# Attention on one NeuronCore: one batch of value matmuls for each chunk of queries, the column groups of TensorE holding the two halves of the keys

## The chip, the core and the metric

The kernel runs on one core of one Trainium2 chip. A core has a matrix engine (TensorE, PE in the profile; its weight loads are listed as PEld), VectorE (DVE), ScalarE (ACT), GpSimd (POOL) and SyncE (SP), which run beside each other and wait for one another by semaphores. Matrix products land in PSUM, which has eight banks of 512 fp32 columns; everything else on the chip lies in SBUF. The metric is the device time in microseconds of one execution; shown is the median of three.

## The reference

Two transformer layers over 4096 tokens of width 256. What the change touches is the attention of the first one, with 16 heads of width 16. The names `k` and `q` are exchanged in the scores, so the softmax of a row runs over what the code calls queries:

```python
q = _split_heads(x @ Wq.T + bq)
k = _split_heads(x @ Wk.T + bk)
v = _split_heads(x @ Wv.T + bv)
scores = jnp.einsum('hbnd,hbmd->hbnm', k, q) * SCALE
attn = jax.nn.softmax(scores, axis=-1)
out = jnp.einsum('hbnm,hbmd->hbnd', attn, v)
```

For each head this is a 4096 by 4096 matrix of scores, its row maxima, its exponentials, and their product with the values and with ones (numerator and denominator). The rest of the layer, and a second layer with linear attention and a mixture of 64 small experts, follow.

## The kernel before

`attention_phase` takes the heads in 8 pairs and the 4096 key columns in 8 blocks of 512 (`TB`), which makes 64 steps. In a step the 4096 query rows go by in 32 chunks of 128 (`MC`), numbered c. The two heads of a pair are e = 0 and e = 1. They live in different halves of the partitions of `QST` and `KST` (rows 0 to 63 and 64 to 127).

For each chunk TensorE does three things. `unit_a` (L624) makes scores with keys on the partitions, 128 by 512, for both heads, and does so ahead of time for a later block; DVE takes their maxima (L719), and the maxima of a whole block travel through POOL (`shift_parts`) and a DMA into two extra rows of `KST`. `unit_s` (L636) makes scores with queries on the partitions, the maxima subtracted by those extra rows; ACT takes their exponential (L696) into one of 8 slots of `PR`. There are only three PSUM banks for it (`SB`), so the matmul number v waits for the exponential number v-3 (`s_before`); from v = 3 to v = 4 the bank repeats at once, so number 4 of a step waits for exponential 3. `values` (L646) multiplies `PR` by the values and by ones (32 columns of weights, `VH`), which accumulates over the chunks in the one bank `PV`.

The order on TensorE is written out in `step`. In each q it issues S for head 0, two matmuls of A (head 1, head 0), and S for head 1. After every second q (odd ones) comes a batch of values for two older chunks: four matmuls of 512 columns that fill the four column groups of 32: head by chunk parity. These matmuls are in plain fp32, and the trace records each as two loads and two matmuls; A and S are of the type fp32r, and recorded once. At the end of a step `PV` holds even and odd chunks in different partitions. ACT copies it to `OS` (L707), POOL moves half of it to other partitions by DMA (L763), adds (L766) and stores it (L773).

The next step's first value matmul waits until `PV` has been copied (`pv_read`). `exp` waits with `p_free` until the slot of `PR` is free again, once for two chunks.

Of the kernel before, what the change touches and what calls it, by code (L numbers as in the profile page):

```python
# [13 lines left out]
F32 = mybir.dt.float32  # L14
# [6 lines left out]
P = 128  # L21
# [3 lines left out]
TB = 512  # L25
# [471 lines left out]
SCALE = 1.0 / D ** 0.5  # L497
LEAD = 8
EXPS = 2 * MC
PVS = MC // 2  # L500
S_BANKS = 3
K_SLOTS = 4
P_SLOTS = 8
# [14 lines left out]
def attention_phase(nc, d, K, V_all):  # L518
# [5 lines left out]
    with ExitStack() as ctx:  # L524
# [7 lines left out]
        PM = sb("PM", [P, 2, 2, TT, NB], F32)  # L532
        neg = sb("neg", [P, 2, 2 * TT], F32)
        NM = sb("NM", [P, 2, PARTS, 2 * TT], F32R)
        OS = sb("OS", [P, 2, TB], F32)
        OG = sb("OG", [P, TB], F32)
        O2 = sb("O2", [P, TB], F32)
        A = ps("A", [P, 4, TB])
        SB = ps("SB", [P, S_BANKS, TB])
        PV = ps("PV", [P, TB])  # L540
# [5 lines left out]
        p_free, os_free, pv_read = sem("p_free"), sem("os_free"), sem("pv_read")  # L546
        neg_ready, neg_high, neg_low = sem("neg_ready"), sem("neg_high"), sem("neg_low")
        shift_loaded = [sem(f"shift_loaded{i}") for i in range(2)]
        groups_moved, o_stored = sem("groups_moved", from_zero=True), sem("o_stored", from_zero=True)
        LOAD = 16 * 2 * len(K_PARTS)  # L550
        SHIFT = 16 * 2 * PARTS
        P_AHEAD = P_SLOTS // 4

        def in_steps(eng, body):

# [9 lines left out]
        with nc.Block() as block:  # L565
# [52 lines left out]
            @block.tensor  # L618
            def _(pe):
                def unit_a(u, e, nb, slot):  # L620
                    i, j = divmod(u, NB)
                    rows = slice(e * HALF, e * HALF + STACK)
                    keys = KST[rows, nb % K_SLOTS, :].rearrange("r (p i) -> r i p", i=TT)[:, i, :]
                    return nc.tensor.matmul(A[:, u % 2 * 2 + e, :], keys, QST[rows, slot, j * TB:(j + 1) * TB],  # L624
                                            start=True, stop=True)

                def units_a(b, u, nb, slot):
                    pe.wait_ge(a_free, count(b * MC + (u + 1)))
                    unit_a(u, 1, nb, slot)
                    unit_a(u, 0, nb, slot).then_inc(a_done, 1)  # L630

                def unit_s(t, c, e, nb, slot):
                    v = 2 * c + e
                    rows = slice(e * HALF, e * HALF + ROWS)
                    pe.wait_ge(s_free, count(t * EXPS + (s_before(v) + 1 + S_BANKS)))
                    nc.tensor.matmul(SB[:, s_bank(v), :], QST[rows, slot, c * P:(c + 1) * P],  # L636
                                     KST[rows, nb % K_SLOTS, :], start=True, stop=True).then_inc(s_done, 1)

                def values(t, k, slot):
                    if k == 0:  # L640
                        pe.wait_ge(pv_read, count(t))
                    pe.wait_ge(s_free, count(t * EXPS + (4 * k + 4 + S_BANKS)))
                    for r in range(4):
                        c, e = 2 * k + r // 2, r % 2
                        at = HALF * e + 2 * HD * (c % 2)
                        mm = nc.tensor.matmul(PV[at:at + 2 * HD, :], VH[:, slot, e, c, :],  # L646
                                              PR[:, (2 * c + e) % P_SLOTS, :], start=(k == 0), stop=(k == PVS - 1))
                    mm.then_inc(p_free, 1)

                def step(two, hp, nb):  # L650
                    t = number(two, hp, nb)
                    for q in range(2, MC + 2):
                        ahead, u = divmod(q + LEAD, MC)
                        ahead += 1
                        past, a_nb = divmod(nb + ahead, NB)
                        if u == 0:
                            block = hp * NB + nb + ahead
                            pe.wait_ge(k_loaded[a_nb % K_SLOTS], count((two * 4 + (block // K_SLOTS + 1)) * LOAD))
                            if a_nb == 0:
                                pe.wait_ge(q_loaded[1 - hp], count((two + (hp + 1) // 2 + 1) * LOAD))  # L660
                        s_t, s_nb, s_slot = t, nb, hp
                        if q >= MC:
                            s_t, s_nb, s_slot = t + 1, (nb + 1) % NB, 1 - hp if nb == NB - 1 else hp
                        if q == MC:
                            block = hp * NB + nb + 1
                            pe.wait_ge(shift_loaded[s_nb % 2], count((two * 8 + (block // 2 + 1)) * SHIFT))
                        unit_s(s_t, q % MC, 0, s_nb, s_slot)
                        units_a(t + ahead, u, a_nb, 1 - hp if past else hp)
                        unit_s(s_t, q % MC, 1, s_nb, s_slot)
                        if q % 2 == 1:  # L670
                            if q == 3 and nb == 0:
                                pe.wait_ge(vh_ready, count(two * 4 + (hp * 2 + 2)))
                            values(t, q // 2 - 1, hp)

                pe.wait_ge(rows_set, count(1))
                pe.wait_ge(q_loaded[0], count(LOAD))
                pe.wait_ge(k_loaded[0], count(LOAD))
                for u in range(MC):
                    units_a(0, u, 0, 0)
                pe.wait_ge(k_loaded[1], count(LOAD))  # L680
                for u in range(LEAD):
                    units_a(1, u, 1, 0)
                pe.wait_ge(shift_loaded[0], count(SHIFT))
                for q in range(2):
                    unit_s(0, q, 0, 0, 0)
                    units_a(1, q + LEAD, 1, 0)
                    unit_s(0, q, 1, 0, 0)
                in_steps(pe, step)

            @block.scalar  # L690
            def _(act):
                def exp(t, v):
                    if v % 4 == 0:
                        act.wait_ge(p_free, count(t * PVS + (v // 4 + 1)))
                    act.wait_ge(s_done, count(t * EXPS + (v + 1)))
                    nc.scalar.activation(PR[:, v % P_SLOTS, :], SB[:, s_bank(v), :], ACT.Exp,  # L696
                                         scale=SCALE).then_inc(s_free, 1)

                def step(two, hp, nb):
                    t = number(two, hp, nb)  # L700
                    for v in range(4, EXPS):
                        exp(t, v)
                    for v in range(4):
                        exp(t + 1, v)
                    act.wait_ge(p_free, count((t + 1) * PVS + P_AHEAD))
                    act.wait_ge(os_free, count(t + 1))
                    nc.scalar.copy(OS[:, nb % 2, :], PV[:, :]).then_inc(pv_read, 1)  # L707

                act.sem_inc(s_free, S_BANKS)
                for v in range(4):  # L710
                    exp(0, v)
                in_steps(act, step)
# [27 lines left out]
            def _(pool):  # L740
# [12 lines left out]

                def step(t, pair, hp, nb, next_pair):
                    if next_pair is not None:
                        pool.wait_ge(p_free, count(t * PVS + P_AHEAD))
                        alone(pool, passed)
                        values_of(next_pair, 1 - hp)
                    shift_parts(t + 1, (nb + 1) % 2)
                    pool.wait_ge(pv_read, count(t + 1))  # L760
                    alone(pool, passed)
                    for e in range(2):
                        pool.dma_start(OG[HALF * e:HALF * e + 2 * HD, :],  # L763
                                       OS[HALF * e + 2 * HD:HALF * (e + 1), nb % 2, :]).then_inc(groups_moved, 16)
                    pool.wait_ge(groups_moved, (t + 1) * 32)
                    nc.gpsimd.tensor_tensor(O2[0:P - 2 * HD, :], OS[0:P - 2 * HD, nb % 2, :], OG[0:P - 2 * HD, :],  # L766
                                            ALU.add).then_inc(os_free, 1)
                    pool.wait_ge(os_free, count(t + 3))
                    alone(pool, passed)
                    for e in range(2):  # L770
                        for j, name in enumerate(("NUM", "DEN")):
                            at = HALF * e + HD * j
                            pool.dma_start(d[name][bass.ds(pair * (2 * HD) + e * HD, HD), nb * TB:(nb + 1) * TB],  # L773
                                           O2[at:at + HD, :]).then_inc(o_stored, 16)
                    pool.wait_ge(o_stored, (t + 1) * 64)

                pool.sem_inc(p_free, P_AHEAD)
                pool.sem_inc(os_free, 2)
                nc.gpsimd.memset(VH[:, :, :, :, HD:2 * HD], 1.0).then_inc(ones_set, 1)
                nc.gpsimd.memset(OG[:, :], 0.0).then_inc(ones_set, 1)  # L780
                pool.wait_ge(ones_set, count(2))
                values_of(0, 0)
                shift_parts(0, 0)
                with pool.Fori(0, HPAIRS // 2 - 1) as two:
# [1177 lines left out]
```

## Time and profile before

| | |
|---|---|
| median of 3 runs | 5071.61 us (5069.26 to 5081.78) |
| profiled execution | 5077.41 us, span 5075.5 us |
| busy PE, DVE, ACT, POOL (whole span) | 4705.6, 3645.4, 3173.7, 394.2 us |
| attention: first to last copy of `PV` | 296.2 to 2962.3 us, 63 steps |
| one undisturbed step | 41.88 us |

A step can be read off the copies of `PV`, of which there is one in each. PE's busy time counts matmuls that overlap, and the ends of matmuls are modelled, so a PE that is busy everywhere may still be waiting. What it waits for is read from the weight loads (PEld) that come before the matmuls. The granted clock 1.00 in the profile is 2.4 GHz, and 0.5 is 1.2 GHz.

### The profile page before, as it was taken

What the parts mean: (1) busy time and instruction counts of PE and PEld (TensorE: products, weight loads), DVE (VectorE), ACT (ScalarE), POOL (GpSimd) and SP (SyncE); (2) the same over time, 40 slices, a digit from 0 to 9 for tenths busy, and PEclk for the clock granted to TensorE, in tenths of its full rate; (3) what the DMA queues carried; (4) which work ended last, traced back from release to release, by engine and by line L of the source; (5) the groups of instructions that cost most, each with busy time, mean ns of one, the idle gap of its engine ahead of it and who ended that gap; (6) DMA issues with size and microseconds to landing.
All of it is one profiled execution on the core that took longest, in us unless ns stands there. A gap on an engine that the chain in (4) does not pass through costs nothing. (4 is left out here: it accounts for less than half of the span.)

```text
span 5075.5 us, 80926 instructions
## 1 busy us (share of the span) xinstructions
PE 4705.6 (93%) x24956; PEld 2773.9 (55%) x24956; DVE 3645.4 (72%) x3695; ACT 3173.7 (63%) x5605; POOL 394.2 (8%) x866
## 2 busy tenths in 40 slices
PE   6699999999999999999999959999885399999999
PEld 4344444444444444444444437777654177777777
DVE  4789999899998999998999965565455444444444
ACT  3178778788887787787878744444473344444444
POOL 0001111111111111111111100000000000000000
PEclk8699999999999999999999979999997699999999
DMA  4310100100101001001010020000001400000000
GB/s 146 96 16 12 26 12 12 22 13 13 25 12 24 12 12 25 13 13 23 12 25 12 13 81 25 33 25 17 23 21 46 114 6 11 12 12 12 12 12 13
DMA packets 145888, 135.28 MB, mean 27 GB/s; under 512 B 83360, under 2 KB 102192, under 8 KB 144720
## 3 DMA queue, kind: packets, MB, share of 16 engines
q1 hardware_dynamic: 133296, 114.48, 9.1%
q0 software_dynamic: 12288, 16.80, 1.6%
q8 instruction: 185, 3.03, 0.3%
q14 instruction: 119, 0.97, 0.1%
HBM read 80.33 MB, written 41.94 MB: 24 GB/s over the span
## 5 line engine op out<-in xcount | busy, mean ns | idle before, releaser
L719 DVE TENSOR_REDUCE PM<-A 128x2 f32<-128x1024 f32 x2090 | 2460.9, 1221 | 292.9 <-PE A L624 292.9
L696 ACT ACTIVATE PR<-SB 128x512 f32<-128x512 f32 x4100 | 2118.2, 605 | 548.0 <-PE SB L636 539.7
L636 PE MATMUL SB<-KST,QST 50*128 50x512 f32 x4100 | 1508.6, 449 | 20.3 <-issue 8.4
L636 PEld LDWEIGHTS SB<-KST,QST 50*128 50x128 f32 x4100 | 699.9, 191 | 1186.7 <-ACT PR L696 1158.5
L624 PE MATMUL A<-QST,KST 48*128 48x512 f32 x4180 | 1273.1, 484 | 37.5 <-DMA QST<-QS 24.7
L646 PE MATMUL PV<-PR,VH 128*32 128x512 f32 x8192 | 1098.8, 609 | 0.0
L624 PEld LDWEIGHTS A<-QST,KST 48*128 48x128 f32 x4180 | 764.3, 306 | 106.9 <-DVE PM L719 43.0
L1860 DVE TENSOR_TENSOR m_h_lo<-m_h_full,m_h_hi 128x512 fp32r<-128x512 f32 x320 | 221.7, 693 | 285.3 <-ACT m_h_hi L1765 285.0
L1765 ACT CAST m_h_hi<-m_h_full 128x512 fp32r<-128x512 f32 x320 | 198.5, 620 | 245.5 <-DVE m_h_full L1857 243.4
L1857 DVE TENSOR_TENSOR m_h_full<-m_h_full,m_c 128x512 f32<-128x512 f32 x256 | 175.3, 685 | 235.2 <-ACT m_h_full L1759 204.8
L646 PEld LDWEIGHTS PV<-PR,VH 128*32 128x32 f32 x8192 | 161.5, 108 | 252.5 <-issue 163.4
L1759 ACT ACTIVATE m_h_full<-m_h,m_b 128x512 f32<-128x512 f32 x256 | 175.8, 687 | 195.1 <-PE m_h L58 194.4
L1071 DVE SCALAR_TENSOR_TENSOR chosen<-gate_out,h_ps 128x512 f32<-128x512 f32 x128 | 87.2, 681 | 181.1 <-PE h_ps L58 181.1
L1010 ACT ACTIVATE h_full<-chosen,b 128x512 f32<-128x512 f32 x128 | 92.4, 722 | 198.0 <-DVE chosen L1071 197.2
L56 PE MATMUL m_h<-ln_hi,moe_w_hi 128*128 128x512 f32 x512 | 208.7, 408 | 0.0
L57 PE MATMUL m_h<-ln_lo,moe_w_hi 128*128 128x512 f32 x512 | 202.8, 396 | 0.0
L56 PE MATMUL m_y<-m_h_hi,moe_w_hi 128*128 128x512 f32 x512 | 201.9, 394 | 0.0
L58 PE MATMUL m_h<-ln_hi,moe_w_lo 128*128 128x512 f32 x512 | 201.8, 394 | 0.0
L58 PE MATMUL m_y<-m_h_hi,moe_w_lo 128*128 128x512 f32 x512 | 201.5, 394 | 0.0
L57 PE MATMUL m_y<-m_h_lo,moe_w_hi 128*128 128x512 f32 x512 | 200.3, 391 | 0.0
L1080 DVE TENSOR_TENSOR h_lo<-h_full,h_hi 128x512 fp32r<-128x512 f32 x192 | 131.3, 684 | 71.6 <-ACT h_hi L1012 71.3
L1656 POOL CAST pick_pair<-pick 128x128 fp32r<-128x128 f32 x256 | 81.7, 319 | 1003.9 <-PE m_c L1678 1002.0
(283 smaller groups left out, 5187.4 us busy)
## 6 DMA issues: line engine op xcount, KB each, us to landing
QST<-QS SPq DMA_DIRECT2D x54, 256.0 KB, 8.4
KST<-KS SPq DMA_DIRECT2D x402, 32.0 KB, 1.8
QS<-parts SPq DMA_DIRECT2D x16, 512.0 KB, 2.8
KS<-parts SPq DMA_DIRECT2D x16, 512.0 KB, 2.8
OG<-OS POOLq DMA_DIRECT2D x128, 64.0 KB, 1.9
m_x<-X3T SPq DMA_DIRECT2D x16, 512.0 KB, 3.7
KST<-NM SPq DMA_DIRECT2D x260, 2.0 KB, 2.0
x_tok<-in_L_attn_x SPq DMA_DIRECT2D x8, 512.0 KB, 4.7
```

Source lines behind the costliest of these rows:

```text
L56: nc.tensor.matmul(out, w[0], x[0], start=first, stop=False)
L57: nc.tensor.matmul(out, w[0], x[1], start=False, stop=False)
L58: return nc.tensor.matmul(out, w[1], x[0], start=False, stop=last)
L624: return nc.tensor.matmul(A[:, u % 2 * 2 + e, :], keys, QST[rows, slot, j * TB:(j + 1) * TB], start=True, stop=True)
L636: nc.tensor.matmul(SB[:, s_bank(v), :], QST[rows, slot, c * P:(c + 1) * P], KST[rows, nb % K_SLOTS, :], start=True, stop=True).then_inc(s_ ...
L646: mm = nc.tensor.matmul(PV[at:at + 2 * HD, :], VH[:, slot, e, c, :], PR[:, (2 * c + e) % P_SLOTS, :], start=(k == 0), stop=(k == PVS - 1))
L696: nc.scalar.activation(PR[:, v % P_SLOTS, :], SB[:, s_bank(v), :], ACT.Exp, scale=SCALE).then_inc(s_free, 1)
L719: nc.vector.tensor_reduce(PM[:, par, :, i, j:j + 1], A[:, u % 2 * 2:u % 2 * 2 + 2, :], AX.X, ALU.max).then_inc(a_free, 1)
L1759: nc.scalar.activation(h_full[:, c % RING, :], h_ps[:, c % 2, :], ACT.Silu, bias=bias).then_inc(full_ready, 1)
L1765: nc.scalar.copy(h[0][:, c % RING, :], h_full[:, c % RING, :]).then_inc(hi_ready, 1)
L1857: nc.vector.tensor_tensor(h_full[:, c % RING, :], h_full[:, c % RING, :], c_ps[:, c % 2, :], ALU.mult).then_inc(kept_ready, 1)
L1860: nc.vector.tensor_tensor(h[1][:, c % RING, :], h_full[:, c % RING, :], h[0][:, c % RING, :].bitcast(F32), ALU.subtract).then_inc(lo_ready, 1)
```

## The change

The batch of values comes in every q and takes one chunk. The four column groups now hold head by half of the 512 keys (`HB` = 256). Both halves use the same weights, so the weights are loaded into two column groups each. Even and odd chunks meet in the same partitions, and so nothing is left to add: the DMA between partitions, POOL's addition and their buffers go, and the results are stored straight from `OS` in pieces half as wide. `PV` uses 256 columns of its bank.

```diff
-PVS = MC // 2
+HB = TB // 2
...
-        P_AHEAD = P_SLOTS // 4
+        P_AHEAD = P_SLOTS // 2
...
-                def values(t, k, slot):
-                    if k == 0:
+                def values(t, c, slot):
+                    if c == 0:
                         pe.wait_ge(pv_read, count(t))
-                    pe.wait_ge(s_free, count(t * EXPS + (4 * k + 4 + S_BANKS)))
-                    for r in range(4):
-                        c, e = 2 * k + r // 2, r % 2
-                        at = HALF * e + 2 * HD * (c % 2)
-                        mm = nc.tensor.matmul(PV[at:at + 2 * HD, :], VH[:, slot, e, c, :],
-                                              PR[:, (2 * c + e) % P_SLOTS, :], start=(k == 0), stop=(k == PVS - 1))
+                    pe.wait_ge(s_free, count(t * EXPS + (2 * c + 2 + S_BANKS)))
+                    for e in range(2):
+                        for b in range(2):
+                            at = HALF * e + 2 * HD * b
+                            mm = nc.tensor.matmul(PV[at:at + 2 * HD, 0:HB], VH[:, slot, e, c, :],
+                                                  PR[:, (2 * c + e) % P_SLOTS, b * HB:(b + 1) * HB],
+                                                  start=(c == 0), stop=(c == MC - 1))
                     mm.then_inc(p_free, 1)
...
-                        if q % 2 == 1:
-                            if q == 3 and nb == 0:
-                                pe.wait_ge(vh_ready, count(two * 4 + (hp * 2 + 2)))
-                            values(t, q // 2 - 1, hp)
+                        if q == 2 and nb == 0:
+                            pe.wait_ge(vh_ready, count(two * 4 + (hp * 2 + 2)))
+                        values(t, q - 2, hp)
...
-                    if v % 4 == 0:
-                        act.wait_ge(p_free, count(t * PVS + (v // 4 + 1)))
+                    if v % 2 == 0:
+                        act.wait_ge(p_free, count(t * MC + (v // 2 + 1)))
...
-                    act.wait_ge(p_free, count((t + 1) * PVS + P_AHEAD))
+                    act.wait_ge(p_free, count((t + 1) * MC + P_AHEAD))
                     act.wait_ge(os_free, count(t + 1))
-                    nc.scalar.copy(OS[:, nb % 2, :], PV[:, :]).then_inc(pv_read, 1)
+                    nc.scalar.copy(OS[:, nb % 2, :], PV[:, 0:HB]).then_inc(pv_read, 1)
...
                     for e in range(2):
-                        pool.dma_start(OG[HALF * e:HALF * e + 2 * HD, :],
-                                       OS[HALF * e + 2 * HD:HALF * (e + 1), nb % 2, :]).then_inc(groups_moved, 16)
-                    pool.wait_ge(groups_moved, (t + 1) * 32)
-                    nc.gpsimd.tensor_tensor(O2[0:P - 2 * HD, :], OS[0:P - 2 * HD, nb % 2, :], OG[0:P - 2 * HD, :],
-                                            ALU.add).then_inc(os_free, 1)
...
+                        for b in range(2):
+                            for j, name in enumerate(("NUM", "DEN")):
+                                at = HALF * e + 2 * HD * b + HD * j
+                                pool.dma_start(d[name][bass.ds(pair * (2 * HD) + e * HD, HD),
+                                                       nb * TB + b * HB:nb * TB + (b + 1) * HB],
+                                               OS[at:at + HD, nb % 2, :]).then_inc(o_stored, 16)
+                    pool.wait_ge(o_stored, (t + 1) * 128)
+                    pool.sem_inc(os_free, 1)
```

On TensorE, two chunks in the middle of a step stood like this before (SB is S, A is A, PV the values):

```order
L636 MATMUL SB<-KST,QST 128x512
L628 REGISTER_ALU
L624 MATMUL A<-QST,KST 128x512 x2
L635 REGISTER_ALU
L636 MATMUL SB<-KST,QST 128x512
L635 REGISTER_ALU
L636 MATMUL SB<-KST,QST 128x512
L628 REGISTER_ALU
L624 MATMUL A<-QST,KST 128x512 x2
L635 REGISTER_ALU
L636 MATMUL SB<-KST,QST 128x512
L646 MATMUL PV<-PR,VH 32x512 x4
```

In the changed kernel one chunk stands like this at the same place, and the next one follows in the same way:

```order
L634 MATMUL SB<-KST,QST 128x512
L626 REGISTER_ALU
L622 MATMUL A<-QST,KST 128x512 x2
L633 REGISTER_ALU
L634 MATMUL SB<-KST,QST 128x512
L644 MATMUL PV<-PR,VH 32x256 x4
```

The work between two batches of values has become half as long, and there are twice as many batches of half the width. TensorE goes from the row halves (A and S) to the column groups (PV) and back once in a chunk instead of once in two.

On POOL the end of a step stood like this before, from the maxima of the next block to the last store:

```order
L749 CAST NM<-neg 128x8
L751 TENSOR_TENSOR NM<-neg,NM 128x8
L763 DMA OG<-OS 32x512 x2
L765 REGISTER_ALU
L766 TENSOR_TENSOR O<-OS,OG 96x512
L768 REGISTER_ALU
L773 ISA
L773 DMA NUM<-O 16x512
L773 DMA DEN<-O 16x512
```

Now it reads as follows, where the last three rows stand four times:

```order
L747 CAST NM<-neg 128x8
L749 TENSOR_TENSOR NM<-neg,NM 128x8
L764 ISA
L764 DMA NUM<-OS 16x256
L764 DMA DEN<-OS 16x256
```

Two DMAs and an addition are gone, and four stores have become eight of half the size.

## Rows read from the trace of the kernel before

**Rows 1.** The page, part 1: busy time of each engine over the span.

```profile
PE 4705.6 (93%) x24956; PEld 2773.9 (55%) x24956; DVE 3645.4 (72%) x3695; ACT 3173.7 (63%) x5605; POOL 394.2 (8%) x866
```

**Rows 2.** Busy time by stretch: an undisturbed step, three where the loop turns, the attention.

```profile
core 0: us, PE busy (x) PEld busy (x) DVE busy (x) ACT busy (x) POOL busy (x), PEclk, DMA share, GB/s
1478.84:1520.72 41.88, 41.79 (x258) 19.00 (x259) 37.95 (x34) 33.55 (x65) 4.66 (x9) 1.00 0.06 13
925.06:975.71 50.65, 46.62 (x258) 20.81 (x259) 37.90 (x34) 33.66 (x66) 5.81 (x11) 0.87 0.27 42
1604.56:1655.17 50.61, 46.52 (x258) 20.82 (x259) 37.89 (x34) 33.67 (x66) 5.83 (x11) 0.87 0.30 42
2284.05:2333.44 49.39, 45.17 (x258) 20.33 (x259) 37.90 (x34) 33.65 (x66) 5.82 (x11) 0.90 0.29 43
297.00:2962.30 2665.30, 2645.68 (x16123) 1202.01 (x16121) 2388.72 (x2079) 2112.87 (x4095) 300.45 (x579) 0.99 0.09 16
```

**Rows 3.** Waits in the attention, 297 to 2962.3 us, longest totals first.

```profile
engine line waited for: us in total, times, longest us
POOL NM L749 <- DVE neg L726: 1291.3, 63, 22.0
PEld SB L636 <- ACT PR L696: 1139.8, 1966, 1.9
POOL OG L763 <- ACT OS L707: 824.9, 63, 13.3
```

**Rows 4.** Timeline of two chunks in the middle of a step.

```profile
start us, us, engine line op out<-in xcount [idle before <-releaser]
1500.85 0.49 PE L636 MATMUL SB<-KST,QST 50*128 50x512 f32 x1
1501.27 0.16 PEld L646 LDWEIGHTS PV<-PR,VH 128*32 128x32 f32 x8 [0.24 <-issue]
1501.27 1.07 PE L646 MATMUL PV<-PR,VH 128*32 128x512 f32 x8
1502.26 0.50 PE L636 MATMUL SB<-KST,QST 50*128 50x512 f32 x1
1502.80 2.07 ACT L696 ACTIVATE PR<-SB 128x512 f32<-128x512 f32 x4 [0.54 <-PE SB L636]
1503.04 2.36 DVE L719 TENSOR_REDUCE PM<-A 128x2 f32<-128x1024 f32 x2 [0.25 <-PE A L624]
1503.45 0.18 PEld L636 LDWEIGHTS SB<-KST,QST 50*128 50x128 f32 x1 [0.29 <-ACT PR L696]
1503.88 0.16 PEld L646 LDWEIGHTS PV<-PR,VH 128*32 128x32 f32 x8 [0.25 <-ACT PR L696]
1504.87 0.18 PEld L636 LDWEIGHTS SB<-KST,QST 50*128 50x128 f32 x1 [0.84 <-ACT PR L696]
```

**Rows 5.** PE's timeline of 1502.0:1502.3, then of 1502.72:1502.74: second PV wave, S for head 1.

```profile
1501.72 0.61 PE L646 MATMUL PV<-PR,VH 128*32 128x512 f32 x4
...
1502.73 0.40 PE L636 MATMUL SB<-KST,QST 50*128 50x512 f32 x1
```

**Rows 6.** PE's timeline of 1469.3:1470.0, where that S waits for nothing.

```profile
1469.48 0.40 PE L636 MATMUL SB<-KST,QST 50*128 50x512 f32 x1
1469.81 0.64 PE L646 MATMUL PV<-PR,VH 128*32 128x512 f32 x4
```

**Rows 7.** PE's timeline at half the clock, after the loop has turned.

```profile
935.08 1.93 PE L646 MATMUL PV<-PR,VH 128*32 128x512 f32 x8
936.95 0.79 PE L636 MATMUL SB<-KST,QST 50*128 50x512 f32 x1
936.95 1.22 PE L624 MATMUL A<-QST,KST 48*128 48x512 f32 x2
937.56 1.03 PE L636 MATMUL SB<-KST,QST 50*128 50x512 f32 x2
938.42 0.79 PE L636 MATMUL SB<-KST,QST 50*128 50x512 f32 x1
939.14 1.93 PE L646 MATMUL PV<-PR,VH 128*32 128x512 f32 x8
```

**Rows 8.** Fp32 matmuls of 128 columns in the second layer: ns min/median/max, first and last start.

```profile
L1357 PE MATMUL kv_ps<-V,k_tok x128: 275/275/347, 3809.0 to 3823.2; 128*128 128x128 f32 x128
```

**Rows 9.** Groups by line: POOL's work at the end of a step, and ACT's copy.

```profile
L766 POOL TENSOR_TENSOR O<-OS,OG 96x512 f32<-96x512 f32 x64 | 81.4, 1272 | 176.0 <-DMA OG<-OS 176.0
L763 POOL DMA_DIRECT2D OG<-OS x128 | 66.3, 520 | 837.9 <-ACT OS L707 837.9
L773 POOL DMA_DIRECT2D NUM<-O x128 | 63.7, 497 | 59.6 <-POOL O L766 44.2 <-issue 11.3
...
L707 ACT COPY OS<-PV x64: 585/587/588, 296.2 to 2962.3; 128x512 f32<-128x512 f32 x64
```

More of the change, by code:

```diff
@@ L534, in attention_phase @@
         NM = sb("NM", [P, 2, PARTS, 2 * TT], F32R)
-        OS = sb("OS", [P, 2, TB], F32)
-        OG = sb("OG", [P, TB], F32)
-        O2 = sb("O2", [P, TB], F32)
+        OS = sb("OS", [P, 2, HB], F32)
         A = ps("A", [P, 4, TB])
@@ L548, in attention_phase @@
         shift_loaded = [sem(f"shift_loaded{i}") for i in range(2)]
-        groups_moved, o_stored = sem("groups_moved", from_zero=True), sem("o_stored", from_zero=True)
+        o_stored = sem("o_stored", from_zero=True)
         LOAD = 16 * 2 * len(K_PARTS)
         SHIFT = 16 * 2 * PARTS
-        P_AHEAD = P_SLOTS // 4
+        P_AHEAD = P_SLOTS // 2
         def in_steps(eng, body):
@@ L755, in step @@
                     if next_pair is not None:
-                        pool.wait_ge(p_free, count(t * PVS + P_AHEAD))
+                        pool.wait_ge(p_free, count(t * MC + P_AHEAD))
                         alone(pool, passed)
@@ L762, in step @@
                     for e in range(2):
-                        pool.dma_start(OG[HALF * e:HALF * e + 2 * HD, :],
-                                       OS[HALF * e + 2 * HD:HALF * (e + 1), nb % 2, :]).then_inc(groups_moved, 16)
-                    pool.wait_ge(groups_moved, (t + 1) * 32)
-                    nc.gpsimd.tensor_tensor(O2[0:P - 2 * HD, :], OS[0:P - 2 * HD, nb % 2, :], OG[0:P - 2 * HD, :],
-                                            ALU.add).then_inc(os_free, 1)
[L768 to L775, printed above, removed]
+                        for b in range(2):
[6 more added lines that the diff above has]
+                    pool.sem_inc(os_free, 1)
                 pool.sem_inc(p_free, P_AHEAD)
@@ L779, in _ @@
                 nc.gpsimd.memset(VH[:, :, :, :, HD:2 * HD], 1.0).then_inc(ones_set, 1)
-                nc.gpsimd.memset(OG[:, :], 0.0).then_inc(ones_set, 1)
-                pool.wait_ge(ones_set, count(2))
+                pool.wait_ge(ones_set, count(1))
                 values_of(0, 0)
```

## The prediction, made before the changed kernel had run

> **What bounds the kernel now.** I read the page first, then busy time by stretch, the waits, and the timeline of one pair of chunks. The page has PE busy for 93% of the span and DVE for 72% [rows 1], over stages that differ. In one step of the attention PE is busy for 41.79 of 41.88 us, DVE for 37.95, ACT for 33.55, POOL for 4.66 [rows 2]. That looks like a PE with nothing to spare. The waits say otherwise: the weight loads of S were held by ACT's exponentials for 1139.8 us in all [rows 3]. Part of that is the ordinary drain between two kinds of work, so the timeline decides [rows 4].
>
> A batch of values starts at 1501.27 and again at 1503.88, which is 2.61 us for two chunks. In between: S (head 0, first chunk) at 1502.26 ends at 1502.76; its exponential starts at 1502.80 (four of them take 2.07 us, the first 0.60); at 1503.45 the fourth S loads its weights, having been held for 0.29 us by that first exponential, because three banks lie under four S; the values start 0.43 later and last 0.99 until the next S at 1504.87. So the period is a chain through two engines, S, exponential, S, values: 0.50 + 0.04 + 0.60 + 0.05 + 0.43 + 0.99 = 2.61. PE alone would need 0.29 less, 2.32 or so; DVE needs 2.36 for its two maxima. The kernel is bound by this chain, with 0.25 us of slack on DVE behind it.
>
> **The change, part by part.**
>
> *The chain.* With values after every chunk the fourth S of a pair is the second S of its own chunk. Its bank is freed by the exponential of the chunk before, which began 0.54 after that chunk's first S and ended at 1.14, before the next chunk begins (below: 1.36). The wait of 0.29 in two chunks goes. What is late next is PE itself.
>
> *PE's part in row halves, per chunk.* From the first load of S to the stream of S for head 1: 1502.26 to 1502.73, 0.47 [rows 4, 5]. It has its loads to hide and they set that pace. From that stream to the start of the values, where nothing is waited for: 1469.48 to 1469.81, 0.33 [rows 6], of which half to two thirds is streaming and the rest emptying the array before the other layout. Together 0.79 or 0.80.
>
> *PE's part in column groups.* The old batch has two waves: 1501.27 to 1501.72 is 0.45, and from there to 1502.26 is 0.54 [rows 4, 5], 0.99 in all. The same batch at half the clock takes 936.95 − 935.08 = 1.87 [rows 7]. With fixed part f and streaming s, f + s = 0.99 and f + 2s = 1.87: s = 0.88, f = 0.11. Rounding and start times leave f between 0.11 and 0.14. At half the width s is halved: 0.44 + 0.11 = 0.55, or 0.43 + 0.14 = 0.57. Does a short matmul cost its share only? 128 fp32 matmuls of 128 columns start within 14.2 us, 0.112 apart [rows 8], a quarter of the 0.45 of a wave of 512. So I keep proportion, and take 0.56. The nearest doubt is 0.005 for each wave.
>
> The Trainium skill says more: "TensorEngine Tiling (Array Packing)", Instruction Overhead, gives each matmul about 60 cycles on top. By that page two more waves for two chunks would cost 0.05 us at 2.4 GHz, an estimate of 51 us over 1024 pairs, and the sum below would be 171 instead of 120. The 0.112 of the trace does not agree with such an addition, at least where matmuls stream.
>
> *Period and step.* 0.795 + 0.56 = 1.355 for a chunk against 1.305 now: 0.05 × 32 = 1.6 us a step. The second switch of layout and its uncovered first load cost 2.71 − 2.32 = 0.39 in two chunks, and the wait that goes gives back 0.29.
>
> *The edge of a step.* S number 4 waits for exponential 3, since they share a bank. It was just in time. Now S number 3 and 4 are neighbours: in the last chunk of a step the first S is done at 0.50, its exponential starts at 0.54, and the one of number 3 is the next behind it, starting 0.49 later ((2.07 − 0.60) / 3) and ending at 1.63; S number 4 can load at 1.68 instead of 1.355. That is 0.33 a step; of the 41.88 of a step now 16 × 2.61 = 41.76 are periods, so the edge cost 0.12 to 0.16. New step: 32 × 1.355 + 0.33 = 43.69, against 41.88 to 41.90. Over 64 steps 1.80 × 64 = 115 us.
>
> *ACT's copy and the first values of a step.* The copy takes 0.587 for 512 columns [rows 9] and less for 256. The last values end at about 1.4, ACT is free at 1.6, so PV is read by 2.2 at the old duration, and the first values come at 1.68 + 0.79 = 2.47. Now they have one chunk of room and not two, and it suffices; without the 0.27 of margin the first wait on it would cost its excess 64 times.
>
> *The other waits.* Slots of PR are freed four chunks back as before, in finer grain: nothing. DVE needs 1.18 in 1.355 and ACT two exponentials, 0.98 in 1.355; both have slack.
>
> *POOL and DMA.* Gone in a step: two DMA issues of 0.52, the landing, an addition of 1.27. Added: four more issues of 0.50 [rows 9], so 4.0 in all and then the landing. Queued behind them is the next block's shift, for which POOL waits 1291.3 us in 63 steps, and for the copy it waits 824.9 [rows 3]. That is 34 us of cover in a step of 42. Nothing either way. If that cover were gone the shift rows of KST would come late, and PE would stop at the start of a step.
>
> *The half-clock stretches.* Three times, where the loop turns, a step takes 49.4 to 50.7 instead of 41.88 [rows 2], part of it at the low clock (1.2 GHz) after PE had stood still. The turn is untouched. At that clock a pair takes 939.14 − 935.08 = 4.06 [rows 7]. A new chunk would take 0.61 to S of head 1, 0.72 more to the values, and 0.11 + 0.88 = 0.99 or a little more: 2.34, so 4.68 a pair. That is 0.62 in each of about ten pairs instead of 0.10: 5 us more.
>
> *Sum.* 115 + 5 = 120 us. The profiled execution, 5077.4, would become 5197. The median shown is 5.8 below it: 5071.6 + 120 = 5192.
>
> **Rivals.**
>
> *Faster: the switch is hidden.* If PE draws the first loads of the other layout under the running matmuls, the switch costs little, the 0.29 remains as gain, and DVE's 1.18 becomes the bound: 32 × 1.18 + 0.33 = 38.1 a step, 3.8 × 64 = 243 us less, 4829. For it: the old chain really had slack on every engine. Against it: on both sides of the values the loads start only when the old work is through (0.33 and 0.54 above, rows that repeat through the attention). It decides below 0.29 us for the switch in two chunks; my value is 0.39, and only 0.10 separates the signs. 7%.
>
> *No change.* The two are equal when a chunk takes 1.30: a row part of 0.74, say, because the matmuls of A find their weights earlier without the second chunk behind them. 5060 to 5087. 5%.
>
> *Much slower: the four groups do not run together.* Two groups now read two halves of one slot and hold equal weights. If they went one after the other, 0.43 would come on top in each of 2048 chunks, 880 us, about 6070. The old groups also read four different streams at once, and nothing in the trace speaks for a conflict. 2%. A smaller form is that issue becomes the limit: a chunk now has 12 recorded pairs of load and matmul, 24 for two against 16. At the 0.112 of rows 8, which is the slowest that issue can be, 12 pairs take 1.34, still under 1.355; with the registers and semaphores between them it could reach 1.42, and then it is (32 × 1.42 + 0.33 − 41.9) × 64 = 248 us, 5320. 6%.
>
> **How the numbers follow.** The forecast has 80%. Its own width comes from the period: 1.335 (row part 0.785, values 0.55) gives 74 us with the half-clock term, 5145; 1.385 (two waves at 0.01 more each and 0.01 at the switch) gives 181, 5253. With 20% for the rivals, of which the near ones touch the ends, I keep 5138 to 5255. About 0.3% (15 us) can be told from no change here. Slower 88%, same 5%, faster 7%.
>
> **What would show it.** In the changed profile a batch of values should start every 1.355 us, and last 0.56 until the next S load. S of head 1 should wait for no exponential. PE's instructions rise to about 33,100. The copies of PV should lie 43.7 us apart, DVE's idle time before a maximum should grow from 0.25 in two to about 0.17 in one, and at a step's edge S should wait 0.3 us for ACT. I am wrong if the next S begins less than 0.5 us after the values, if the period is that of DVE (1.18), or if ACT's copy holds up the first values.

## The result

The changed kernel takes 5219.34 us (median of four, 5209.97 to 5241.34), the kernel before 5071.87 in the same comparison. The ratio is 1.0285, with a 95% interval from 1.0265 to 1.0306: 147 us slower. 5192 had been forecast, with a range of 5138 to 5255.

The page after, busy time of each engine (compare [rows 1]):

```profile
PE 4839.3 (93%) x33148; PEld 2753.7 (53%) x33148; DVE 3736.8 (72%) x3695; ACT 3269.6 (63%) x5605; POOL 370.1 (7%) x929
```

TensorE has 8192 more recorded matmuls, as the batch of values is cut twice as fine. Shares of busy time have hardly moved. PE's busy time has grown by 133.7 us, but PE counted as busy for 99.8% of a step before as well, its waits included, so this line doesn't tell whether PE works more or waits more, nor in which stage. Busy time by stretch after, with the columns of [rows 2]: an undisturbed step, the three in which the loop turns, and the attention from the first to the last copy of `PV`:

```profile
1534.41:1578.22 43.81, 43.57 (x384) 18.62 (x384) 39.36 (x34) 35.04 (x66) 4.30 (x10) 1.00 0.04 10
955.05:1008.74 53.69, 51.21 (x384) 19.98 (x384) 39.26 (x34) 35.03 (x66) 5.46 (x12) 0.81 0.27 38
1665.83:1732.65 66.82, 64.18 (x384) 22.31 (x384) 39.46 (x34) 35.14 (x66) 5.47 (x12) 0.59 0.22 30
2389.70:2440.79 51.09, 48.29 (x384) 19.48 (x384) 39.27 (x34) 35.04 (x66) 5.47 (x12) 0.87 0.27 39
297.96:3097.90 2799.94, 2777.15 (x24192) 1179.25 (x24192) 2478.92 (x2080) 2208.15 (x4096) 277.20 (x642) 0.98 0.07 13
```

And the same whole stretch of the kernel before:

```profile
296.19:2962.28 2666.09, 2646.49 (x16128) 1202.71 (x16128) 2389.22 (x2080) 2113.66 (x4095) 300.45 (x579) 0.99 0.09 16
```

Between the two profiled executions (5216.5 and 5075.5 us of span) lie 141.0 us. The attention has 133.9 of them. Its three turning steps take 171.6 in place of 150.65, 20.9 more, and the other 60 steps share 112.9, which is 1.88 each. So there are two causes in the attention: a longer step everywhere, and longer turns. The 7.2 us that are left lie before the first and behind the last copy.

The timeline after, two chunks in the middle of a step (columns as in [rows 4]):

```profile
1500.28 0.18 PEld L634 LDWEIGHTS SB<-KST,QST 50*128 50x128 f32 x1 [0.41 <-ACT PR L694]
1500.75 0.40 PE L634 MATMUL SB<-KST,QST 50*128 50x512 f32 x1
1501.07 0.16 PEld L644 LDWEIGHTS PV<-PR,VH 128*32 128x32 f32 x8 [0.37 <-issue]
1501.64 0.18 PEld L634 LDWEIGHTS SB<-KST,QST 50*128 50x128 f32 x1 [0.41 <-ACT PR L694]
1502.11 0.39 PE L634 MATMUL SB<-KST,QST 50*128 50x512 f32 x1
1502.42 0.16 PEld L644 LDWEIGHTS PV<-PR,VH 128*32 128x32 f32 x8 [0.36 <-issue]
1502.99 0.18 PEld L634 LDWEIGHTS SB<-KST,QST 50*128 50x128 f32 x1 [0.41 <-ACT PR L694]
```

From 1500.28 to 1501.64 to 1502.99 a chunk takes 1.36 and 1.35. The part in row halves is 1501.07 − 1500.28 = 0.79, the values 0.57, and S for head 1 streams 0.47 after the chunk's first load. It no longer waits for an exponential: the wait of 0.29 before its load in [rows 4] has no row here. The 0.41 before the first S is put down to ACT, but it begins where the loads of the values end, and covers the streaming of the values and the emptying of the array. That is how such a wait is told from a real one, and a run below confirms it: with exponentials and maxima of half the width, the waits of this kind in all steps come to 836.5 us in place of 863.3:

```profile
PEld SB L634 <- ACT PR L694: 863.3, 2013, 0.8
PEld SB L634 <- ACT PR L694: 836.5, 2009, 0.8
```

Most of the 27 us between them is the edge of a step, of which more below.

### The profile page after: what moved, and what is told of

Its sections match the earlier page's. It is cut to its first block and busy times, and to the rows that moved or that the text cites. A ratio compares the mean times of both kernels' runs of the same rounds, so it can differ in the third digit from the quotient of the medians.

```text
span 5216.5 us, 98698 instructions
## 1 busy us (share of the span) xinstructions
PE 4839.3 (93%) x33148; PEld 2753.7 (53%) x33148; DVE 3736.8 (72%) x3695; ACT 3269.6 (63%) x5605; POOL 370.1 (7%) x929
## 5 line engine op out<-in xcount | busy, mean ns | idle before, releaser
L717 DVE TENSOR_REDUCE PM<-A 128x2 f32<-128x1024 f32 x2090 | 2554.5, 1226 | 337.6 <-PE A L622 101.9
L694 ACT ACTIVATE PR<-SB 128x512 f32<-128x512 f32 x4100 | 2225.0, 595 | 603.0 <-PE SB L634 603.0
L634 PE MATMUL SB<-KST,QST 50*128 50x512 f32 x4100 | 1777.1, 451 | 23.7 <-ACT PR L694 15.8
L622 PE MATMUL A<-QST,KST 48*128 48x512 f32 x4180 | 1550.2, 519 | 37.1 <-DMA QST<-QS 24.3
L644 PE MATMUL PV<-PR,VH 128*32 128x256 f32 x16384 | 1328.3, 396 | 0.0
L634 PEld LDWEIGHTS SB<-KST,QST 50*128 50x128 f32 x4100 | 803.6, 197 | 888.4 <-ACT PR L694 879.1
L622 PEld LDWEIGHTS A<-QST,KST 48*128 48x128 f32 x4180 | 861.5, 308 | 57.9 <-DVE PM L717 32.6
L644 PEld LDWEIGHTS PV<-PR,VH 128*32 128x32 f32 x16384 | 324.5, 109 | 760.4 <-issue 760.4
L764 POOL DMA_DIRECT2D NUM<-OS x256 | 126.6, 495 | 878.2 <-ACT OS L705 811.6
```

The source lines that it names most:

```text
L644: mm = nc.tensor.matmul(PV[at:at + 2 * HD, 0:HB], VH[:, slot, e, c, :], PR[:, (2 * c + e) % P_SLOTS, b * HB:(b + 1) * HB], start=(c == 0), ...
L717: nc.vector.tensor_reduce(PM[:, par, :, i, j:j + 1], A[:, u % 2 * 2:u % 2 * 2 + 2, :], AX.X, ALU.max).then_inc(a_free, 1)
```

## The experiments

### The two halves of the change apart

The first version keeps the key halves and issues the values of two chunks together.

```diff
-                        if q == 2 and nb == 0:
-                            pe.wait_ge(vh_ready, count(two * 4 + (hp * 2 + 2)))
-                        values(t, q - 2, hp)
+                        if q % 2 == 1:
+                            if q == 3 and nb == 0:
+                                pe.wait_ge(vh_ready, count(two * 4 + (hp * 2 + 2)))
+                            values(t, q - 3, hp)
+                            values(t, q - 2, hp)
```

> The changed kernel, with the values of two chunks issued together after every second q, as before (16 matmuls of 256 columns in a batch, and half as many switches of layout). Theory (the switch costs): the batch takes 4 x 0.213 + 0.14 = 0.99 us, the period for two chunks is again the chain S, exponential, S, values of 2.61 us, a step 41.9 us, the time 5060 to 5090 us. Rival (the narrow matmuls or their loads cost): each of four waves costs more than its share, and the time stays near 5200 us, with a batch above 1.05 us.

Measured: 5081.0 us against 5080.6 for the kernel before, ratio 1.0001 (0.9991 to 1.0011). Its timeline:

```profile
1500.01 0.59 PEld L644 LDWEIGHTS PV<-PR,VH 128*32 128x32 f32 x16 [0.25 <-ACT PR L696]
1500.01 1.07 PE L644 MATMUL PV<-PR,VH 128*32 128x256 f32 x16
1501.01 0.18 PEld L634 LDWEIGHTS SB<-KST,QST 50*128 50x128 f32 x1 [0.41 <-ACT PR L696]
1502.20 0.18 PEld L634 LDWEIGHTS SB<-KST,QST 50*128 50x128 f32 x1 [0.31 <-ACT PR L696]
1502.62 0.59 PEld L644 LDWEIGHTS PV<-PR,VH 128*32 128x32 f32 x16 [0.24 <-ACT PR L696]
```

Sixteen recorded matmuls of 256 columns take 1.00 us, where eight of 512 took 0.99, and the wait for the exponential before the fourth S is back (0.31). The period is 2.61. The narrow matmuls, their doubled loads and the shorter path through POOL together cost and give nothing here. This version differs from the changed kernel only in when the batches come, and the whole loss is gone. So the loss comes with a batch after every chunk, that is with twice as many switches between the layouts. (The forecast for this run, 5060 to 5090 us with a step of 41.9, was met.)

The second version does the other half alone: a batch after every chunk, but 512 keys in each of two column groups. Shown is the batch itself; it is issued in every q, as in the changed kernel, with the semaphore counts that go with it.

```diff
-                    for r in range(4):
-                        c, e = 2 * k + r // 2, r % 2
+                    for r in range(2):
+                        c, e = k, r
...
-                                              PR[:, (2 * c + e) % P_SLOTS, :], start=(k == 0), stop=(k == PVS - 1))
+                                              PR[:, (2 * c + e) % P_SLOTS, :], start=(k < 2), stop=(k >= PVS - 2))
```

> The kernel before, with the values issued after every chunk, but with all 512 keys in each of two column groups (head by chunk parity as before; two groups stand idle in a batch). Theory: a batch costs its streaming of 0.85 and 0.14 fixed whatever the number of groups, a chunk 0.79 + 0.99 = 1.78 us, a step 57.1 us, the time 5072 + 64 x 15.2 = 6045 us, 5990 to 6100. Rival (the four groups share the array's input, so that two of them stream twice as fast): a chunk of 1.36 us, and about 5200 us.

Measured: 6014.79 us, ratio 1.1841 (1.1817 to 1.1865). The timeline shows a batch of four recorded matmuls:

```profile
1500.65 0.14 PEld L646 LDWEIGHTS PV<-PR,VH 128*32 128x32 f32 x4 [0.36 <-issue]
1500.66 1.05 PE L646 MATMUL PV<-PR,VH 128*32 128x512 f32 x4
1501.64 0.18 PEld L636 LDWEIGHTS SB<-KST,QST 50*128 50x128 f32 x1 [0.84 <-ACT PR L695]
1502.43 0.14 PEld L646 LDWEIGHTS PV<-PR,VH 128*32 128x32 f32 x4 [0.38 <-issue]
```

The batch takes 0.99 with two groups at work as it did with four, and a chunk 1.78. So a batch costs its columns and a fixed part, with two groups as with four. This is also what the key halves are for: without them a batch for each chunk costs 934 us, with them 147.

### Is it ACT that bounds the kernel before?

This version leaves out half of each exponential, so its results are not those of the reference; it only shows what ACT's time is worth.

```diff
-                    nc.scalar.activation(PR[:, v % P_SLOTS, :], SB[:, s_bank(v), :], ACT.Exp,
+                    nc.scalar.activation(PR[:, v % P_SLOTS, 0:TB // 2], SB[:, s_bank(v), 0:TB // 2], ACT.Exp,
```

> The kernel before, where each exponential takes only the first 256 of its 512 columns (the other half of PR holds ones). Theory (a chain through ACT bounds the kernel before): the exponential takes 0.38 and not 0.60 us, the period for two chunks falls from 2.61 to 2.39, a step from 41.9 to 38.3 us or a little above, where DVE's 2.36 comes next, and the time to about 4840 us (4820 to 4880). Rival (PE, which is busy 99.8% of a step, is the bound): no change, 5060 to 5085 us.

Measured: 4940.2 us, ratio 0.9728 (0.9712 to 0.9745). The rival, that a PE busy for 99.8% of a step is the bound, is refuted: 140 us go with half of each exponential, on an engine that was idle for a fifth of the step. But the size was wrong. A step takes 39.72, not 38.3:

```profile
1416.95:1456.67 39.72, 39.72 (x258) 18.39 (x258) 37.92 (x34) 22.72 (x66) 4.67 (x9) 1.00 0.07 13
```

The waits of that kernel have a row that was 10 us in the one before:

```profile
PEld A L624 <- DVE PM L719: 131.6, 506, 0.6
```

and one such wait in its timeline, between two batches of values:

```profile
1499.86 3.63 DVE L719 TENSOR_REDUCE PM<-A 128x2 f32<-128x1024 f32 x3 [0.20 <-PE A L624]
1500.49 0.16 PEld L646 LDWEIGHTS PV<-PR,VH 128*32 128x32 f32 x8 [0.25 <-ACT PR L696]
1502.27 0.31 PEld L624 LDWEIGHTS A<-QST,KST 48*128 48x128 f32 x2 [0.25 <-DVE PM L719]
1503.05 0.16 PEld L646 LDWEIGHTS PV<-PR,VH 128*32 128x32 f32 x8 [0.36 <-ACT PR L696]
```

A has two units of banks, and PE now reaches the third unit before DVE has taken the maximum of the first. The load of A is held for 0.25 us, in about half of the pairs of chunks (506 times in 1024). DVE in turn waits for A (0.20 in the first line), and is busy for 37.92 of the 39.72 us. The expectation took DVE's 2.36 for two maxima, 37.8 a step, as the next bound, and left out that PE and DVE wait for each other. That this is the whole of the missing 1.4 us is argued from these rows; no run takes half of the maxima away as well in this kernel. The period from 1500.49 to 1503.05 is 2.56, and without the 0.25 it is 2.31: this is PE alone, which the prediction had put at 2.32. Taking DVE's work away in the kernel before shows the other side.

```diff
-                    nc.vector.tensor_reduce(PM[:, par, :, i, j:j + 1], A[:, u % 2 * 2:u % 2 * 2 + 2, :], AX.X,
+                    nc.vector.tensor_reduce(PM[:, par, :, i, j:j + 1], A[:, u % 2 * 2:u % 2 * 2 + 2, 0:TB // 2], AX.X,
```

> The kernel before, where each maximum takes only the first 256 of its 512 columns for each head. Theory (the chain through PE and ACT sets the period, DVE only follows): no change of the step, 41.9 us, and 5070 to 5088 us. Rival (DVE, busy for 91% of a step, sets it or a share of it): the step falls by 1 us or more, and the time below 5015 us.

Measured: 5066.2 us, ratio 0.9978 (0.9968 to 0.9987), and the step is 41.90 with DVE busy for half of it:

```profile
1465.12:1507.02 41.90, 41.80 (x258) 19.61 (x259) 20.86 (x33) 33.55 (x66) 4.67 (x9) 1.00 0.06 13
```

DVE was no bound of the step, though busy for 91% of it. The 10 us come from elsewhere: the first copy of `PV` comes at 282.58 us instead of 296.19, since DVE had been busy for 45.47 of the 50 us from 200 to 250, with the units of A that go ahead of the first step.

### And the changed kernel?

Here both are cut: the exponentials to 256 columns, as above, and the maxima to 256 of each head.

> The changed kernel, where each exponential takes the first 256 of its 512 columns (the other half of PR holds ones) and each maximum the first 256 columns of each head. Theory (PE alone bounds the chunk, ACT only the edge of a step): a chunk stays at 1.356 us, and only the wait of 0.4 us at the edge of a step goes, 64 times: a step of 43.4 us, 5185 to 5205 us. Rival (ACT or DVE still sets the pace of the changed kernel): a chunk below 1.33 us, and a time below 5150 us.

Measured: 5212.94 us (5175.63 to 5232.77), ratio 1.0276 (1.0248 to 1.0303). That is above the 5185 to 5205 expected, and far from the rival's 5150. The time says little, because its four executions lie 57 us apart. The step is clear:

```profile
1519.51:1562.96 43.45, 43.45 (x386) 18.56 (x386) 22.39 (x33) 24.10 (x65) 4.30 (x10) 1.00 0.05 10
```

43.45 in place of 43.81, with DVE and ACT busy for about half of it. A chunk is as long as before, and only the edge is gone. So between the edges the changed kernel is bound by PE alone, by its streaming and its switches together.

### The edge of a step, and the turns

At the edge of a step in the changed kernel S number 4 waits for exponential 3, as its timeline shows:

```profile
1489.83 0.64 PE L644 MATMUL PV<-PR,VH 128*32 128x256 f32 x8
1490.61 0.37 ACT L705 COPY OS<-PV 128x256 f32<-128x256 f32 x1
1490.72 0.18 PEld L634 LDWEIGHTS SB<-KST,QST 50*128 50x128 f32 x1 [0.74 <-ACT PR L694]
1490.80 0.34 PEld L622 LDWEIGHTS A<-QST,KST 48*128 48x128 f32 x2
1491.58 0.16 PEld L644 LDWEIGHTS PV<-PR,VH 128*32 128x32 f32 x8 [0.36 <-issue]
```

S comes 0.89 after the values and not 0.57, and this chunk takes 1.75 instead of 1.355: an edge of 0.40. The next version gives the banks in another order, in which no number of S follows at once behind the last use of its bank.

```diff
+BANK_ORDER = (0, 1, 2) * 2 + (0, 1) + (0, 2, 1) * 18 + (0, 2)
...
-    return (v if v < 4 else v + 2) % S_BANKS
+    return BANK_ORDER[v]
```

> The changed kernel with another order of the three banks of S over the 64 matmuls of a step. Two numbers of S then follow two places behind the last use of their bank, and none follows it at once. Theory: the wait of S number 4 for exponential 3 at the edge of a step (0.4 us) goes, a step is 32 x 1.356 = 43.4 us and not 43.80, and the time is 20 to 28 us less than that of the changed kernel. Rival: something else stands behind the edge (the copy of PV, the exponentials 0 to 3 ahead of it), and less than 8 us go.

For comparison the changed kernel ran again beside it.

> The changed kernel once more, beside the next three on the same chip. 5210 to 5240 us by its four earlier times. Of its gap to the kernel before, 1.90 us in each of 64 steps is the same in each execution; what differs between executions should be the time at the low clock after the turns of the loop.

Measured: 5194.39 us with the new order (ratio to the kernel before 1.0235, 1.0216 to 1.0254), 5240.47 without it (1.0309, 1.0284 to 1.0334). The step is 43.41, which is 32 × 1.356 and nothing besides:

```profile
1539.88:1583.29 43.41, 43.41 (x386) 18.51 (x386) 39.37 (x34) 35.01 (x66) 4.32 (x10) 1.00 0.05 10
```

The edge accounts for 64 × 0.39 = 25 us of the 46 between the two medians. The rest fits the low clock of the executions: the two in the middle of the repeated run had a mean granted clock of 0.950 and 0.951, the median one with the new order 0.954, and (0.954 − 0.9505) × 5240 is 18 us. Whether the new order had a part in that no run shows, since executions of one kernel differ by as much. The turns of the repeated run:

```profile
956.41:1020.99 64.58, 61.62 (x384) 21.67 (x384) 39.45 (x34) 35.03 (x66) 5.49 (x12) 0.63 0.22 31
1678.04:1731.59 53.55, 51.01 (x384) 19.91 (x384) 39.30 (x34) 35.14 (x67) 5.49 (x12) 0.81 0.27 38
2388.67:2456.71 68.04, 65.56 (x384) 22.28 (x384) 39.46 (x34) 35.05 (x66) 5.49 (x12) 0.57 0.21 29
```

A granted clock of 0.57 over 68.04 us means (1 − 0.57) / 0.5 = 86% of it, or 58 us, at 1.2 GHz. In the kernel before it was 13 us [rows 2, the first turn]. The three turns cost 54.8 us over three normal steps here, 40.2 in the first profile, 25.0 in the kernel before. The 14.6 us between the first two are the 14.7 between the times of these two executions (5232.82 and 5218.13). The other executions fit: the six of the repeated run go from 5206.22 us at a mean clock of 0.959 to 5249.62 at 0.948, and the longer the lower.

I took the load of the next pair's query rows to be the cause of PE's standing still at the turn, since it fills the DMA engines there, and moved it by one block.

```diff
-                    if nb == 0:
+                    if nb == 1:
                         load_q(following, 1 - hp)
```

> The changed kernel, with the load of the next pair's query rows (six DMAs of 256 KB) issued in the second block of a pair and not the first, so that it no longer meets the fetching of instructions where the loop turns. Theory (the load holds up the turn, PE stands still, and the low clock that follows lasts longer in the changed kernel, 20 to 58 us against 10 to 14): the three turns cost less than 5 us each in place of 15 on average, no stretch at 1.2 GHz is left in the attention, and the time is 30 to 45 us below the changed kernel's, near 5190 us, with little spread. What then remains over the kernel before is the 1.90 us of each step. Rival (the turn's stall is the fetching itself): the turns stay as they are, 5210 to 5245 us.

Measured: 5224.07 us (5209.34 to 5250.53), ratio 1.0288 (1.0264 to 1.0311). This theory fell for the changed kernel: about 5190 had been expected by it, 5210 to 5245 by its rival. The turning steps have almost no DMA left in them (0.04 in place of 0.22 to 0.27), and are as long, 169.1 us in all where the two profiles with the early load have 171.6 and 186.2:

```profile
960.52:1014.12 53.60, 51.01 (x384) 19.98 (x384) 39.31 (x34) 35.15 (x66) 5.46 (x12) 0.81 0.04 8
1671.21:1727.63 56.42, 53.98 (x384) 20.48 (x384) 39.28 (x34) 35.05 (x67) 5.47 (x12) 0.76 0.04 8
2384.67:2443.72 59.05, 56.56 (x384) 20.91 (x384) 39.33 (x34) 35.10 (x67) 5.47 (x12) 0.71 0.03 7
```

Its timeline at the first turn shows PE waiting 3 us for nothing that the profile records, and then at the low clock:

```profile
962.97 0.28 PEld L634 LDWEIGHTS SB<-KST,QST 50*128 50x128 f32 x1 [3.06 <-issue]
962.98 0.79 PE L634 MATMUL SB<-KST,QST 50*128 50x512 f32 x1 [2.59 <-issue]
```

So in the changed kernel PE stands still because of the turn itself, and not because of the query rows. That it is the fetching of instructions, as the expectation has it, is a supposition that no run tests.

### Looking for a version that beats both

The key halves in batches of two chunks with the new order of banks:

> The version with key halves and batches of two chunks, with the new order of banks. Theory: a step is 16 periods of 2.605 us, 41.7 us, and the edge (0.12 to 0.16 us) goes, so that the time is 6 to 12 us below that of the kernel before, about 5063 us. Rival: the edge is hidden by the chain anyway, and nothing changes.

Measured: 5073.52 us against 5078.61, ratio 0.9991 (0.9982 to 1.0000). An undisturbed step takes 41.81 in place of 41.87. That is 5 us less where 6 to 12 had been expected, and at the limit of what can be told. The order of banks alone in the kernel before:

> The kernel before with the new order of banks alone. Theory: as in the version with key halves, 6 to 12 us less than before, if the copy of 512 columns of PV does not take the place of the wait; rival: the copy and the exponentials behind it hold the fourth S at the edge, and nothing changes (within 4 us).

Measured: 5078.68 us, ratio 0.9998 (0.9989 to 1.0006), a step of 41.95. Nothing, so the rival had it: in the kernel before something else stands at the edge. The longer copy is the candidate; no run tests it. Then all together, with the late load of the query rows:

> Key halves, batches of two chunks, the new order of banks, and the query rows loaded one block later. Theory: the three turns cost 1 to 2 us and not 8 each, and the time is some 20 us below the same version with the early load (5073), about 5052 us, which would be 0.5% below the kernel before. Rival: the turns stay, 5073 us.

Measured: 5077.51 us, ratio 0.9999 (0.9990 to 1.0009), not the 5052 expected. Its three turns are shorter (45.98, 47.21 and 46.62 us), but five other steps are now 0.5 to 7 us longer, so that the attention takes 2666.1 us, as in the kernel before. These five are steps in which the moved load runs. In the two longest of them PE stands still, for nothing that the profile records, as it does at a turn:

```profile
1997.16 0.50 PE L637 MATMUL SB<-KST,QST 50*128 50x512 f32 x1 [2.62 <-issue]
2677.18 0.79 PE L637 MATMUL SB<-KST,QST 50*128 50x512 f32 x1 [2.33 <-issue]
```

So here the load moved a part of its cost instead of losing it. What it holds up, no run shows. The late load in the kernel before:

> The kernel before with the query rows loaded one block later. Theory: 15 to 22 us less than before, 5056 to 5063 us. Rival: no change.

Measured: 5073.65 us, ratio 0.9990 (0.9981 to 0.9998), with turns of 45.58, 47.74 and 46.10 us. 15 to 22 us less had been expected. The turns are 11 us shorter in all, and 3 us of that show in the time. So in the kernel before the load does have a part in the turn. PE stands still twice at the first turn there (first two lines), and with the late load once (third line):

```profile
927.60 0.50 PE L636 MATMUL SB<-KST,QST 50*128 50x512 f32 x1 [2.68 <-issue]
930.30 0.79 PE L636 MATMUL SB<-KST,QST 50*128 50x512 f32 x1 [1.49 <-ACT PR L696]
929.67 0.49 PE L636 MATMUL SB<-KST,QST 50*128 50x512 f32 x1 [2.42 <-issue]
```

No version that does the whole work beats the kernel before by more than 0.1%.

## Why the prediction was right

*What bounds the kernel before.* Right: the chain S, exponential, S, values. Half of each exponential takes 2.7% off, half of each maximum takes nothing off a step. The waits of the weight loads told this, and the busy time of PE did not.

*The wait of 0.29 goes.* Right, its row is gone.

*The row part and the batch of values.* 0.79 against 0.795, and 0.57 against 0.56. The chunk was forecast at 1.355 and measured at 1.356 (43.41 / 32). The sum held because each part came from a row where nothing was waited for, and the values' fixed part from the same batch at both clocks. The Trainium skill ("TensorEngine Tiling (Array Packing)", Instruction Overhead) gives each matmul an overhead of about 60 cycles, which the prediction read as an addition. The same section says that a matmul of one column takes as long as one of 60, which reads as a least duration. The traces show no addition: four waves of 256 took 1.00 us where two of 512 took 0.99, and by the addition it would have been 0.05 more.

*The edge.* S was forecast at 0.33 late and came 0.32 late. The chunk takes 0.07 more behind it, as A's weights load 0.08 after those of S and not beside them; that was left out. Step: 43.81 against 43.69, so this term came to 1.88 to 1.90 us for a step and 121 in all, not 115.

*The half-clock stretches.* This is the term that was mis-sized: 5 us forecast, 15 in the profile of the changed kernel (20.9 for three steps less 3 × 1.9), and about 30 in the repeated run. At the low clock a chunk takes 2.18 (960.49 to 962.67 in the trace after), less than the 2.34 forecast. The part from S of head 1 to the values was put at 0.72, from an S that had just been held for an exponential and had to load its weights uncovered; at the full clock such an S gives 0.43 and not 0.33 [rows 4, 6]. Here it takes 962.67 − 962.12 = 0.55. What failed is the number of chunks at that clock: I had let the stretches last as long as before, about ten pairs in all. By the granted clock they lasted for 36 us in the three turning steps before, for 88 in the profile after, and for up to 58 us in a single one.

```profile
960.49 1.08 PE L644 MATMUL PV<-PR,VH 128*32 128x256 f32 x8
962.12 0.62 PE L634 MATMUL SB<-KST,QST 50*128 50x512 f32 x1
962.67 1.08 PE L644 MATMUL PV<-PR,VH 128*32 128x256 f32 x8
```

*ACT's copy and POOL.* Right in that they don't show: the copy takes 0.37, its margin was never used, and POOL waits longer for the maxima than before (1574.4 against 1291.3 us).

*DVE.* Its idle time before a maximum is (43.81 − 39.36) / 32 = 0.14, where about 0.17 was forecast: spaced as they are now the maxima take 1.23 each and not 1.18. It was no bound.

*The rest.* Before the first and after the last copy lie 7.2 us more, which no step of the prediction had. Together 121 + 15 + 7 = 143 us, against 141.0 between the two profiles; the 147 of the medians is more because the profiled execution before lay 5.5 us above its median and the one after 1.2 below. So the 27 us that the forecast missed are mainly the turns, the ends and the edge, and they stayed inside a range that had been drawn for the width of a chunk. In that range one sum is off: the 74 us and 5145 of its lower case leave out the 5 us of the half clock, which the upper case has; it should be 79 and 5150.

*The rival that the switch is hidden* asked for less than 0.29 us for a second switch. It costs 2 × 1.356 − 2.32 = 0.39, where 2.32 is PE alone before, found as 2.31 in the version with half exponentials. The key-half version with batches of two chunks shows it from the other side: with the same matmuls and half the switches the whole 147 us are gone.

What stays open is why the low clock lasts so much longer in the kernel with a batch per chunk. The four profiles of kernels with key halves, a batch per chunk and full exponentials have turning steps of 51 to 68 us, where a normal one takes 43.4 to 43.8. Those with batches for two chunks have 46 to 51 beside 41.9. The version with a batch per chunk and 512 columns has 60 to 63 beside 56.7, so the number of switches alone is not it. How long PE stands still doesn't tell either: 2.80 us before 13 us of low clock and 2.48 before 58 in the changed kernel.

## What to carry to other kernels

When two kinds of matmul use different layouts of the array, price the switch from the trace: here each additional round trip cost some 0.39 us of PE's time, and it only pays to switch more often if the wait that this removes is longer (here it was 0.29). An engine that is busy all the time need not be the bound; look at what its weight loads wait for, and take the size of the next bound from a run: here PE and DVE, sharing two units of banks, came to 39.72 us a step where DVE's work alone takes 37.8. A gain or loss that differs between executions of one kernel should be looked for in the granted clock, step by step.

## What had not been expected of the hardware

PE stood still for 2.48 to 2.97 us at each turn, in the two profiles of the changed kernel as in the one before. The clock then fell to 1.2 GHz, and stayed there for anything from 13 to 58 us in the changed kernel, though PE was recorded busy for some 95% of those steps (65.56 of 68.04 us in the longest); in the kernel before it came back within 10 to 14 us each time. A batch of values of given width takes the same time with two column groups at work as with four (0.99 us).
